# Expert layer in two threads: encoder and router share a PSUM bank with the projections

## The reference

```python
x = x + 0.5 * ffn(norm(x))          # ffn1: 128 -> 512 -> 128, gelu, ternary weights, inner norm
x = x + attn0(norm(x))              # small scan with 16 states, gelu gate
x = x + 0.5 * ffn(norm(x))          # ffn2, same weights
x = x + 0.5 * moe(norm(x))          # "moef": encoder 128 -> 256 -> 64, router top 2 of 8 experts,
                                    #   experts 64 -> 128 -> 64, decoder 64 -> 256 -> 128
x = x + mamba(norm(x))              # convolution and projections, 256 channels x 16 states, scan in
                                    #   chunks of 32 positions, output projection
x = x + 0.5 * moe(norm(x))          # "moeb", same weights as moef
```

## Time and profile before

| | us |
|---|---|
| median of 3 runs (lowest to highest) | 1283.71 (1281.35 to 1285.73) |
| profiled execution, its time | 1283.91 |
| its span, first to last instruction | 1281.8 |
| TensorE busy | 1026.1 (80%) |
| VectorE busy | 853.3 (67%) |
| GpSimd busy | 668.1 (52%) |
| ScalarE busy | 649.6 (51%) |
| mean granted TensorE clock, share of full speed | 0.855 |

### The profile page before, as it was taken

One profiled execution on the slowest core, in us unless ns is written; L12 is line 12 of the kernel. 1 busy time (PEld: TensorE's weight loads), 2 busy tenths in 40 slices (PEclk: granted clock), 3 DMA queues, 4 the chain that ended last, 5 costly groups with the idle time before them and its releaser, 6 DMA issues.

```text
span 1281.8 us, 11264 instructions
## 1 busy us (share of the span) xinstructions
PE 1026.1 (80%) x3604; PEld 512.0 (40%) x3604; DVE 853.3 (67%) x1505; ACT 649.6 (51%) x1018; POOL 668.1 (52%) x540
## 2 busy tenths in 40 slices
PE   0456889879898979987988999988877787786855
PEld 0233544445364434443554355443333233332322
DVE  1321323677876798788688867788886779788611
ACT  1133457566677474755667764764542255333111
POOL 0013133576575694766566775756665566465211
PEclk9866788799889878988999988888988789888856
DMA  4000102434344444543544446355646345556120
GB/s 106 0 9 1 75 1 73 167 132 164 143 141 163 165 141 157 173 173 131 200 162 152 163 135 221 129 188 177 243 157 219 131 164 200 203 188 215 68 74 8
DMA packets 55715, 176.60 MB, mean 138 GB/s; under 512 B 7332, under 2 KB 17896, under 8 KB 51560
## 3 DMA queue, kind: packets, MB, share of 16 engines
q1 hardware_dynamic: 55656, 175.89, 39.1%
HBM read 172.99 MB, written 2.88 MB: 137 GB/s over the span
## 4 chain that ended last, share of the span: by engine, by line
PE 52%; DVE 20%; ACT 11%; POOL 9%; issue 4%; SPq 2%; DMA 1%; POOLq 0%; DVEq 0%; ACTq 0%
PE yp L1329 12%; PE mp L1228 5%; DVE hs L876 5%; PE mp L1237 5%; PE fp L1147 4%; PE fp L1153 4%; DVE hs L882 3%; PE fp L1139 3%; PE pp L1271 3%; DVE he L818 2%; ACT L904 2%; PE mp L1203 2%; PE mp L1243 2%; SPq L376 2%; PE mp L1198 2%
## 5 line engine op out<-in xcount | busy, mean ns | idle before, releaser
L622 POOL TENSOR_TENSOR dbu<-du,bcast 128x1024 f32<-128x1024 f32 x128 | 342.7, 2681 | 240.2 <-DVE hs L876 136.0
L876 DVE TENSOR_TENSOR_SCAN hs<-dA,dbu 128x512 f32<-128x512 f32 x256 | 302.6, 1208 | 93.3 <-ACT dA L1095 44.0
L1329 PE MATMUL yp<-hs,ident 128*128 128x512 f32 x512 | 295.3, 709 | 45.9 <-DVE hs L882 45.7
L1095 ACT ACTIVATE dA<-delta,mA 128x496 f32<-128x496 f32 x256 | 168.8, 671 | 173.3 <-DVE hs L876 171.4
L882 DVE TENSOR_TENSOR hs<-hs,bcast 128x1024 f32<-128x1024 f32 x128 | 202.9, 1585 | 3.4
L1329 PEld LDWEIGHTS yp<-hs,ident 128*128 128x128 f32 x512 | 105.6, 222 | 190.6 <-issue 114.6
L1228 PE MATMUL mp<-cont,w_e 64*128 64x512 f32 x256 | 107.0, 792 | 26.5 <-DVE he L818 21.3
L818 DVE SCALAR_TENSOR_TENSOR he<-mp,vectors,he 128x512 f32<-128x512 f32 x128 | 89.8, 742 | 43.7 <-PE mp L1228 34.0
L904 ACT ACT_TABLE_LOAD x75 | 96.2, 1283 | 1.3
L1139 PE MATMUL fp<-f_zT,w 128*128 128x512 f32 x128 | 71.8, 688 | 3.5 <-ACT f_zT L924 2.3
L1237 PE MATMUL mp<-he,w_e 128*64 128x512 f32 x256 | 73.3, 725 | 0.0
(11 more groups left out here) (214 smaller groups left out, 1489.2 us busy)
## 6 DMA issues: line engine op xcount, KB each, us to landing
bcast<-held SPq DMA_DIRECT2D x128, 1024.0 KB, 5.3
he<-gates SPq DMA_DIRECT2D x32, 1024.0 KB, 6.6
xin<-L_attn_x SPq DMA_DIRECT2D x8, 256.0 KB, 2.8
out<-xo SPq DMA_DIRECT2D x8, 256.0 KB, 3.1
held<-bc SPq DMA_DIRECT2D x8, 64.0 KB, 4.9
he<-conv_wT SPq DMA_DIRECT2D x1, 384.0 KB
w<-w1T SPq DMA_DIRECT2D x1, 256.0 KB
he<-w2T SPq DMA_DIRECT2D x1, 256.0 KB
```

The costliest lines, as they stand in the source:

```text
L622: pool.tensor_tensor(out=dbu[:, j % 2, :].rearrange("p (r t) -> p r t", r=2), in0=d, in1=b_n, op=ALU.mult).then_inc(dbu_r.sem, 1)
L876: dve.tensor_tensor_scan(out=hs[:, j % 2, half], data0=dA[:, half], data1=dbu[:, j % 2, half], initial=0.0, op0=ALU.mult, op1=ALU.add).the ...
L1095: act.activation(out=dst, in_=src, func=ACT.Exp, scale=mA[:, c, n:n + 1]).then_inc(dA_r.sem, 1)
L1329: last = pe.matmul(yp[:, :], lhsT=ident[:, :], rhs=hs[:, j % 2, r * SEQ:(r + 1) * SEQ], start=(k == 0 and r == 0), stop=(k == PAIRS - 1 an ...
```

## The change

The expert layer's thread M and the projections' thread P are replaced by A and B. A runs in `pp` and has, in the order `A_TURNS`, for k = 0, 1, ...: the front of moef k, mout k - 2, the front of moeb k - 2, mpre k. B runs in `mp` and has the backs of the turns in the order of `M_TURNS`, which is now moef 0, moef 1, moef 2, moeb 0, moef 3, moeb 1, ... (moeb two batches behind moef, where it was three). Encoder products and tanhs alternate in the one bank, with a step of their own each. `mz`, `mzT` and `pz`, `pzT` become one pair `az`, `azT`; the decoder's tanh gets its own tile `s2`. A back's first expert product waits for `cont` and for the `dd` of the back before it, not for the front's `gT`; the bias product waits for `gT`. The copy to `cont` waits for the expert sum of two turns earlier. The other engines' generators are split in the same way, and all orders are new; TensorE's is shown.

```diff
-LEAD = 3
-M_TURNS = [(stage, i) for k in range(BATCH + LEAD) for stage, i in (("moef", k), ("moeb", k - LEAD))
-           if 0 <= i < BATCH]
-ALONE = 16
-M_HALVES = [half for m in range(2 * BATCH + 1) for half in
-            ((("front", m), ("back", m)) if m < ALONE else (("front", m),) if m == ALONE else
-             (("front", m), ("back", m - 1))) if half[1] < 2 * BATCH]
-P_TURNS = [(stage, i) for k in range(BATCH + 1) for stage, i in (("mpre", k), ("mout", k - 1)) if 0 <= i < BATCH]
+
+A_TURNS = [(stage, i) for k in range(BATCH + 2) for stage, i in
+           (("moef", k), ("mout", k - 2), ("moeb", k - 2), ("mpre", k)) if 0 <= i < BATCH]
+M_TURNS = [turn for turn in A_TURNS if turn[0] in ("moef", "moeb")]
...
     "PE":
-        "FFFFFFFFFFFFFFFFFFFFFFFMFMFMFMFFFFMFMMFMFMFMMMFMFFFFFFFFFPPFPMFMPFMPMPFPFFPMFFMFMMFMFSMMFSMFMSFSFSFF"
-        "SFFFFFPSPSPFMFMFFSMFFFFFMSSPPMPMPFFSMFSMPMFMMFSMFSMSFFPFFFFFSPSPPMFSMFMSMPFFMMFFFFSSMFMMSMMSMFPMFSPF"
-        "SSPFPMMSMSMFSFFFMFFFFSMFSMPMMFMMSMPSPMPSFPFFPSPSFMFFMFMPMSPFMSMSMFFMSMFMMSMFMFSFSMSMFFMSMFFFFMFMSMSM"
-        "FMFMMSMSMSPFFFFFFFSSPMPMSMFSFMSPFPMMPSFMPMPMPMMSFSMFMSFFFFFSFFSMSMMSFMFPFMFMFFFFSFSMSMPMPMMFSMFSSMPS"
-        "FPFPPMSMPMFMSFPFMFMSFSFFFMSMFMSMMSMSMSPSMMSMPMPSPMSMPPSPSPPMSMSMMMSMSMSSSMMMSMSMMSPMMMMMSMSMSSSMPSMP"
-        "MSMSPMPMPPSPMMPMSMMSMSMSSSMMMSMPMMSSMMMMMSMSMSSSSMMMSMSMMSSSMMMMMSMSMSPMMMMMMMMMMMMM",
+        "FFFFFFFFFFFFFFFFFFFFFFFAFAFAFAFAFFFFABFFBFBBBFBBFBFFFFFFFFAAFAFAFFAFAFFFAFAFFAFSAFASAABSFFAFFSFFFFFS"
+        "BBBBSBSBFSBFFFSSFFFFFASASAASAFSFASAFSAFAAASAFSAFSFFBAAFFFFFSSBABABABBSBSFBSFAFSAFBFFAFFFASASASABAFBA"
+        "FSABASBBSFSBFBAAAFSFASASFFBFAFFASFFSBABAASBABSBSBFABFFFBAFFFFSFSASASABASAFAFASBSFBASBBFBBAAASFASFASF"
+        "FBFAFFASFFSBSBABABBSABSBFAFABSFFFFAFFFASASASABASABFABFSBASBSFBBFAAAAFSAFSFFBAFAFFFFSSABASABABABFBSAB"
+        "SBFSFFBFFFFFSABASASAFBFASAFSBBABAFBSBFSAFASFAFASABFFFAFASFSBASABABABASBBABSBSSBBABABASASABASABSBASSS"
+        "AASAASABSAASSBSBAASABABABSBSABBSBSBSABASASASABASABASBABSASASAABSASSASSSBSBSBSBSBSBSBSAAAAABAABBBBBBB",
...
             def front(m, stage, i):
                 yield True
-                normed(mn, m, mz, xm_input(stage, i), mzn)
-                yield True
-                turned(mzT[:, :], mps[0], mzt_ps, mzt, m)
-                yield True
-                table(ACT.Tanh)
-                if m >= 1:
-                    act.wait_ge(dec_ps.sem, dec_ps.at(m - (1 if m <= ALONE else 2), 1))
+                normed(mn, m, az, xm_input(stage, i), mzn)
+                yield True
+                turned(azT[:, TAPS - 1:], pp[:, :], mzt_ps, mzt, m)
                 for c in range(EC):
+                    yield True
+                    table(ACT.Tanh)
                     act.wait_ge(enc_ps.sem, enc_ps.at(m, c + 1))
-                    act.activation(out=s1[:, c, :], in_=mps[(c + 1) % 2], func=ACT.Tanh, bias=b_enc[:, c:c + 1],
+                    act.activation(out=s1[:, c, :], in_=pp[:, :], func=ACT.Tanh, bias=b_enc[:, c:c + 1],
                                    scale=0.5).then_inc(s1r.sem, 1)
                 yield True
                 act.wait_ge(cont_ps.sem, cont_ps.at(m, 1))
-                act.activation(out=cont[:, m % 2, :], in_=mps[0], func=ACT.Identity,
+                if m >= 2:
+                    act.wait_ge(eoT_ps.sem, eoT_ps.at(m - 2, 1))
+                act.activation(out=cont[:, m % 2, :], in_=pp[:, :], func=ACT.Identity,
                                bias=b_s2c[:, :]).then_inc(contr.sem, 1)
...
-                act.activation(out=gT[:, m % 2, :], in_=mps[0][0:EXPERTS, :], func=ACT.Copy).then_inc(gT_r.sem, 1)
+                act.activation(out=gT[:, m % 2, :], in_=pp[0:EXPERTS, :], func=ACT.Copy).then_inc(gT_r.sem, 1)
...
-            def free(half, m):
-
-                done = gT_r if half == "front" else ddr
-                pe.wait_ge(done.sem, done.at(m, 1))
-
-            def front(m, stage, i):
-                yield True
-                before = M_HALVES[M_HALVES.index(("front", m)) - 1] if m else None
-                if m:
+            def free(stage, i):
+
+                if stage == "mpre":
+                    pe.wait_ge(dtb_r.sem, dtb_r.at(i, IC))
+                elif stage == "mout":
+                    pe.wait_ge(xm.sem, xm.at(i, 1))
+                else:
+                    pe.wait_ge(gT_r.sem, gT_r.at(M_TURNS.index((stage, i)), 1))
+
+            def front(m, before):
+                yield True
+                if before:
                     free(*before)
-                turn(mps[0], mz, mzn, mzt_ps, m * TILES)
+                turn(pp, az, mzn, mzt_ps, m * TILES)
                 yield True
                 pe.wait_ge(mzt.sem, mzt.at(m, 1))
                 for c in range(EC):
-                    pe.matmul(mps[(c + 1) % 2], lhsT=w_enc[:, c * P:(c + 1) * P], rhs=mzT[:, :],
+                    if c:
+                        yield True
+                        pe.wait_ge(s1r.sem, s1r.at(m, c))
+                    pe.matmul(pp[:, :], lhsT=w_enc[:, c * P:(c + 1) * P], rhs=azT[:, TAPS - 1:],
                               start=True, stop=True).then_inc(enc_ps.sem, 1)
                 yield True
                 pe.wait_ge(s1r.sem, s1r.at(m, EC))
                 for c in range(EC):
-                    last = pe.matmul(mps[0], lhsT=w_s2c[:, c, :], rhs=s1[:, c, :],
+                    last = pe.matmul(pp[:, :], lhsT=w_s2c[:, c, :], rhs=s1[:, c, :],
                                      start=(c == 0), stop=(c == EC - 1))
                 last.then_inc(cont_ps.sem, 1)
                 yield True
                 pe.wait_ge(contr.sem, contr.at(m, 1))
                 for q in range(TILES):
-                    last = pe.matmul(mps[1][:, q * EXPERTS:(q + 1) * EXPERTS],
+                    last = pe.matmul(pp[:, q * EXPERTS:(q + 1) * EXPERTS],
                                      lhsT=cont[0:MOE, m % 2, q * P:(q + 1) * P], rhs=w_r[:, :], start=True, stop=True)
                 last.then_inc(route_ps.sem, 1)
...
-            def back(m, stage, i):
-                before = M_HALVES[M_HALVES.index(("back", m)) - 1]
+            def back(m):
                 for e in range(EXPERTS):
                     if e % 2 == 0:
                         yield True
                     if e == 0:
-                        free(*before)
+                        pe.wait_ge(contr.sem, contr.at(m, 1))
+                        if m:
+                            pe.wait_ge(ddr.sem, ddr.at(m - 1, 1))
                     if e >= 2:
                         pe.wait_ge(her.sem, her.at(m, e - 1))
                     half = slice(MOE * (e % 2), MOE * (e % 2 + 1))
...
                               start=True, stop=True).then_inc(he_ps.sem, 1)
                 yield True
                 pe.wait_ge(her.sem, her.at(m, EXPERTS))
+                pe.wait_ge(gT_r.sem, gT_r.at(m, 1))
                 pe.matmul(mps[0][0:MOE, :], lhsT=b_e2[:, :], rhs=gT[:, m % 2, :], start=True, stop=False)
...
-                        last = pe.matmul(mps[0][:, q * P:(q + 1) * P], lhsT=s1[:, c, q * P:(q + 1) * P],
+                        last = pe.matmul(mps[0][:, q * P:(q + 1) * P], lhsT=s2[:, c, q * P:(q + 1) * P],
...
                 yield True
-                if before is not None and before[0] == "mout":
-                    pe.wait_ge(xm.sem, xm.at(before[1], 1))
-                elif before is not None:
-                    pe.wait_ge(dtb_r.sem, dtb_r.at(before[1], IC))
-                turn(pp, pz, pzn, pzt_ps, i * TILES)
+                free(*before)
+                turn(pp, az, pzn, pzt_ps, i * TILES)
```

173 lines of the change are left out of this document (92 added, 81 removed).

## The result

The changed kernel takes 1270.7 us (median of 4 runs, 1267.6 to 1274.2), the kernel before 1284.5 beside it (4 runs, 1281.4 to 1285.7). The ratio is 0.9897 (95%: 0.9864 to 0.9929), a gain of 13.8 us where 29.7 was forecast. A repetition on another chip gave 1272.6 and 0.9894. The profiled execution took 1267.6 us, the fastest of its four, and its span is 1265.9; TensorE's mean granted clock is 0.865 (before 0.855).

A forecast was written before the change was run, and what follows sets the result against it. The prediction took thread M's chain of expert turns to be full to the end, with TensorE nearly the bound early. Filling 232 + first five scans 640 + last three 310 + tail 69.8, plus 2.1, gave 1254 us; range 1226 to 1296.

The forecast's parts named there:

- The filling: Time up to the first scan step: 4 us less, 232 us for 236, with bounds of 0 and -11.5.
- the first five scans: Scans of the first five batches, beside the F threads: 640 us for 648, at a TensorE busy share of 0.925.
- the tail: After the last scan, batch 7's last expert turn: 1 us more for the shared encoder bank, 69.8 us for 68.8.
- the last three scans: Scans of the last three batches: 310 us for 329, at a TensorE busy share of 0.86, halfway between 0.79 and 0.925.
- the clock: TensorE's granted clock in the last scan: 0.75 for 0.81 would make it 5 us longer; left out of the sum.
- a higher busy share: TensorE in the scans: the only source of gain, 0.925 for 0.904 in the first five, 0.86 for 0.79 later.
- Early expert products: A back's first two expert products may start before the router ends: -2 us in the tail at most, counted at nothing.
- Rival 1: A's chain sets the time between deltas, 127 us or more for 120; 1306 us total at 130; chance 0.16.
- Rival 2: The order changes but TensorE's busy share does not, TensorE being the bound: around 1286 us; chance 0.16.
- Rival 3: M's chain was the whole bound of the scans, shares rise to 0.96 and 0.925: around 1215 us; chance 0.08.
- The SyncE queue: Gate loads waiting for the previous back's expert sum hold up bcast loads: priced at 0, some 5 us a batch if it bites.

## Why the prediction was right and wrong

**The filling is the step that failed.** It stood at 236 - 4 = 232 with 0 and -11.5 as bounds; it was +8 (243.7 for 235.6). The 7 us of TensorE's work did leave, but the bounds were made of work alone: a loss by the new order of the remaining entries, or by a lower clock, was put at nothing without a reason. Batch 0's projections did get 4.5 us shorter. Its front got 3.7 longer, since its gates' transposes stand behind F's sum of squares, and its back 9.4, partly since its second expert pair stands behind F's products and partly at a clock of 0.76 for 0.83 in the stretch. That the clock has a good part is shown: with it at 0.88 the way from the norm to the first scan step is 111.3 us for 119.0. That the first step then falls on the forecast's 232.0 is luck, since 4 us of it are won ahead of that way. Of the 16.7 us between forecast (1254) and median (1270.7), 12 are this term; 4 are the first five scans, 1 the tail, -3 the last three scans, and 3 the distance of the median from the profiled execution.

The prediction had named the clock and left it out of its sum. It looked for it in the last scan (0.75 for 0.81), where it stayed at 0.81 with 61.6 us of work; it fell in the filling, where no term asked for it.

**The first five scans, 640 forecast, 644 measured, for a reason that fell.** The step "a higher busy share" said 0.925; it was 0.894, under the old 0.904. The busy time was 575.8 us and not 592, for two reasons. The five windows hold 2159 matmuls where before's had 2205; each group at its mean duration in before, that is 0.7% less work, where the list of letters gave 1% more. And the sum multiplied by the old busy time per price (0.904), which holds only at the old clock (0.92 on the mean of the five for 0.90). The misses, in share, work and price, cancelled by luck: 592/0.925 = 640, 575.8/0.894 = 644.

**The last three, 310 and 307.** The halfway share of 0.86 was too high here too (251.6/307 = 0.82), with a busy time of 252 for 266. That these scans had room is borne out: the last one takes 80 us for 109. That M's chain had left it there fits, but no run isolates it: the one meant for that, before without gates, took nothing off M's chain in the scans.

**The tail, 69.8 and 70.9.** Right; the run without gates shows 8 us of it to be the gates' way through DRAM, the reason for which the early products were counted at nothing there.

**Early expert products at nothing** was wrong in the scans by some 3% in the list as it is (without them 1307.5). It hurt the prediction only in its reasons: the scans' gain of 26 us was ascribed to the shares, and with this list and without this part it wouldn't be there.

**Rival 1, A's chain.** Its time from delta to delta was nearly right: 124.7 us on the mean, under its 127 and over the chain's 120, with pauses of up to 12.5 us between the scans. The parts were mis-sized, projections 34 for 44 and the handover 11.4 for 1, and these nearly cancel. Whether the chain is the bound is not shown. A delay of 4.8 us on it came through by three fourths, as the theory wants, but in before, off M's chain, it came through as well; and of the two attempts to shorten the chain one left TensorE's step where it was and the other took away 8 us of waiting in eight scans.

**Rival 2, the share stays,** had the premise right (0.870 for 0.867) and the time wrong (1286), since it too kept the clock. **Rival 3** (shares of 0.96 and 0.925) fell with 0.894 and 0.82. What the prediction says against it, four scans near 0.92, was misread: the earlier trace rows has 0.89 to 0.91 in four and 0.925 in one. **The SyncE queue** at 0: GpSimd waits 121.1 us for bcast where before it was 104.1, by the groups of the two pages, and VectorE 20.9 for gates where it was 9.3. Both grew, by 2 us a scan and 12 in all, far under the 5 us a batch that the prediction gave if it bites; whether any of it reached the time is open.

**What stays open.** Two removals of work brought a fourth or less of themselves (145 us of TensorE's work 15, 67 of VectorE's 12 to 16), the removal of 20.9 us of waits for gates brought 13, and a delay put in came through by three fourths or more. One reading is that queues of fixed order were fitted to certain durations: a late step holds up what stands behind it, an early one finds its neighbours where they were, as the norm that came 16 us early did. It is a reading, and no run tests it by itself. Which single wait sets the 124.7 us isn't settled, nor why small changes of order cost 1 to 2.7%; in five reordered kernels the mean clock was 0.851 to 0.867 around the 0.865 of after, so that it is no more than a part of it.

The best kernel of the study is the changed one with the useless products of the filling: 1260.9 us, 0.9809 (0.9776 to 0.9842) of before, 0.9% better than the change alone.

## What to carry to other kernels

Give a stretch where TensorE has gaps a term for the clock and one for the new order of what is left in it, each with a sign of its own: moving work out of it can cost more than the work. Don't take a busy share for nearness to a bound while the granted clock is below 1; here, at 0.865, 145 us of matmuls less were 63 us of busy time less. In queues of fixed order, price a step by what stands behind it, and test the parts of a change singly (the one counted at nothing carried this one, in its list). Before a run that takes a wait away, read in the trace how long the wait is, and after one that moves a step, where the step behind it starts: three of the runs here took away much less than they were built for.

## What the runs showed of the hardware

That 29 products whose results nobody reads, put into gaps between 51 and 222 us, make a kernel 12 us faster was not expected, nor that they do nothing for the kernel before. Nor was it that TensorE's busy time falls by 63 us where 145 us of matmuls go. And in the tail a clock of 0.82 for 0.63 shortened it by 3.6 us where 12 were expected, and nothing of that shows in the medians.
